# A two-layer conditioned kernel on Trainium2: another order of blocks in head and tail, a sixth buffer, and three moved steps in the loop

## What is computed

```python
# layer L0: styles scale the input channels, demod the outputs
styles = w @ (affine_w * gain).T + affine_b
dcoefs = rsqrt(sum((weight * styles)**2, axis=2) + 1e-08)
y = einsum('blc,oc->blo', x * styles, weight) * dcoefs
x = x + clip(y + bias, -256, 256)
# attention over the heads of one token: q = k = v = kx
kx = modulated_linear(x, s, k_aff_w, k_aff_b, k_w, k_b).reshape(B, N, 16, 32)
scores = einsum('bnhd,bnjd->bnhj', kx, kx) / sqrt(32)
out = einsum('bnhj,bnjd->bnhd', softmax(scores), kx).reshape(B, N, 512)
x = x + modulated_linear(out, s, o_aff_w, o_aff_b, o_w, o_b)
```

## Time and profile before

| what | value |
|---|---|
| median of the runs | 777.33 us |
| profiled execution, its own time | 782.16 us |
| its span (first to last instruction) | 780.4 us |
| granted TensorE clock, mean | 0.967 |
| busy: PE, VectorE, ScalarE | 93%, 71%, 65% |
| DMA queue of SP, share of 16 engines | 78.4% |

### The profile page before, as it was taken

One profiled execution on the slowest core, in us unless ns is written; L12 is line 12 of the kernel. 1 busy time (PEld: TensorE's weight loads), 2 busy tenths in 40 slices (PEclk: granted clock), 3 DMA queues, 4 the chain that ended last, 5 costly groups with the idle time before them and its releaser, 6 DMA issues.

```text
span 780.4 us, 21455 instructions
## 1 busy us (share of the span) xinstructions
PE 723.8 (93%) x8848; PEld 702.9 (90%) x8848; DVE 553.3 (71%) x1040; ACT 510.1 (65%) x1036; POOL 11.7 (1%) x8
## 2 busy tenths in 40 slices
PE   5999788999999999999999999999999999998676
PEld 4999678989999999999999999999999999997566
DVE  4555765778877777787787777778788777776562
ACT  4265547767776766777676677777677776675353
POOL 2300000000000000000000000000000000000000
PEclk9799898999999999999999999999999999998888
DMA  8028686898889988888878988888888889876763
GB/s 297 28 63 198 160 194 185 225 220 218 202 211 227 230 219 230 227 218 209 214 199 216 220 239 223 228 220 223 221 198 210 220 228 232 213 185 151 167 180 108
DMA packets 235778, 157.15 MB, mean 201 GB/s; under 512 B 143265, under 2 KB 225185, under 8 KB 235681
## 3 DMA queue, kind: packets, MB, share of 16 engines
q1 hardware_dynamic: 235680, 155.78, 78.4%
HBM read 71.85 MB, written 67.11 MB: 178 GB/s over the span
## 4 chain that ended last, share of the span: by engine, by line
DMA 37%; PE 28%; SPq 13%; DVE 9%; ACT 9%; issue 4%; DVEq 0%; ACTq 0%
PE lin_ps L388 21%; DMA yr<-y_turned 14%; DMA k_st<-k_turned 12%; DMA k_turned<-kx 8%; SPq L235 7%; SPq L225 4%; DVE k_rhs L676 4%; ACT y_hi L477 3%; ACT kx L468 3%; PE s_ps L426 3%; PE y_ps L444 2%; PE y_ps L411 2%; DVE p_bd L738 1%; DMA v_turned<-k_rhs 1%; SPq L249 1%
## 5 line engine op out<-in xcount | busy, mean ns | idle before, releaser
L388 PE MATMUL lin_ps<-x_hi,w_hi 128*128 128x256 f32 x1024 | 300.6, 294 | 21.5 <-ACT x_hi L477 14.5
L388 PE MATMUL lin_ps<-x_hi,w_lo 128*128 128x256 f32 x1024 | 292.8, 286 | 0.0
L388 PE MATMUL lin_ps<-x_lo,w_hi 128*128 128x256 f32 x1024 | 292.6, 286 | 0.0
L388 PEld LDWEIGHTS lin_ps<-x_hi,w_hi 128*128 128x128 f32 x1024 | 196.9, 192 | 35.1 <-issue 29.3
L388 PEld LDWEIGHTS lin_ps<-x_lo,w_hi 128*128 128x128 f32 x1024 | 197.8, 193 | 0.0
L388 PEld LDWEIGHTS lin_ps<-x_hi,w_lo 128*128 128x128 f32 x1024 | 197.2, 193 | 0.0
L388 PE MATMUL lin_ps<-y_hi,w_hi 128*128 128x256 f32 x512 | 147.6, 288 | 12.0 <-DVE y_lo L626 7.9
L388 PE MATMUL lin_ps<-y_lo,w_hi 128*128 128x256 f32 x512 | 146.7, 287 | 0.0
L388 PE MATMUL lin_ps<-y_hi,w_lo 128*128 128x256 f32 x512 | 146.5, 286 | 0.0
L477 ACT ACTIVATE x_hi<-x,style 128x256 fp32r<-128x256 f32 x256 | 115.1, 499 | 36.9 <-DVE x L697 27.1
L626 DVE SCALAR_TENSOR_TENSOR x_lo<-x,style,x_hi 128x256 fp32r<-128x256 f32 x256 | 109.5, 480 | 10.7 <-ACT x_hi L477 10.6
(11 more groups left out here) (48 smaller groups left out, 667.8 us busy)
## 6 DMA issues: line engine op xcount, KB each, us to landing
x<-xT SPq DMA_DIRECT2D x32, 512.0 KB, 6.0
k_turned<-kx SPq DMA_DIRECT2D x32, 512.0 KB, 3.6
k_st<-k_turned SPq DMA_DIRECT2D x128, 128.0 KB, 4.0
k_bd<-k_rhs SPq DMA_DIRECT2D x128, 128.0 KB, 2.4
v_turned<-k_rhs SPq DMA_DIRECT2D x32, 512.0 KB, 6.6
k_v<-v_turned SPq DMA_DIRECT2D x128, 128.0 KB, 3.7
y_turned<-y SPq DMA_DIRECT2D x128, 128.0 KB, 3.2
yr<-y_turned SPq DMA_DIRECT2D x32, 512.0 KB, 5.0
```

The lines of the kernel that those rows point to most:

```text
L388: mm = pe.matmul(lin_ps[:, n % NLB, 0:T], w[:, k, m * P:(m + 1) * P], r[:, k, :], start=(q == 0), stop=(q == len(passes) - 1))
```

## The change

Head: L0(4) and L0(5) come earlier on PE (L0(4) ahead of scores(1), L0(5) ahead of pv(1)), and O(1), K(5), scores(4) and pv(3) are written out; the loop begins at i = 6 instead of 5. Since L0(5) now comes before `finish(0)`, there are six buffers of x1, and `l0_out(c)` waits for `finish(c-6)` instead of `finish(c-5)`. SP's, ScalarE's and VectorE's heads are reordered with it. Tail: the loop ends one iteration earlier (i = 29); K(30) comes right after two blocks of O(26), L0(31) right after K(30), ahead of scores(29) and pv(28), and K(31) before the other two blocks of O(26). Loop: VectorE makes the first half of x1 ahead of `normalise`, the first low half right after, `turn_k` after both halves of x1, `spread_probabilities` after both low halves; ScalarE runs `spread_some` after both high halves of x1 instead of before `l0_out(i, 3)`. No instruction's work changes, and there are as many of each kind.

```diff
-    NX1 = DEPTH + 1
+    NX1 = DEPTH + 2
+    FIRST_LOOP = DEPTH + 2
...
-            + blocks(K, 2) + one("scores", 1) + blocks(K, 3) + one("pv", 0) + blocks(L0, 4) + one("scores", 2)
-            + blocks(K, 4) + one("pv", 1) + blocks(O, 0) + one("scores", 3) + one("pv", 2))
-        pe_program += [step for i in range(DEPTH + 1, last) for step in pe_steps(i)]
+            + blocks(K, 2) + blocks(L0, 4) + one("scores", 1) + one("pv", 0) + blocks(K, 3) + one("scores", 2)
+            + blocks(L0, 5) + one("pv", 1) + blocks(K, 4) + blocks(O, 0) + one("scores", 3) + one("pv", 2)
+            + blocks(O, 1) + blocks(K, 5) + one("scores", 4) + one("pv", 3))
+        pe_program += [step for i in range(FIRST_LOOP, last - 1) for step in pe_steps(i)]
         pe_program += (
-            blocks(L0, last) + blocks(O, last - 4, [0, 1]) + blocks(K, last) + one("scores", last - 1)
-            + one("pv", last - 2) + blocks(O, last - 4, [2, 3]) + blocks(O, last - 3) + one("scores", last)
-            + one("pv", last - 1) + blocks(O, last - 2) + one("pv", last) + blocks(O, last - 1) + blocks(O, last))
+            blocks(L0, last - 1) + blocks(O, last - 5, [0, 1]) + blocks(K, last - 1) + blocks(L0, last)
+            + one("scores", last - 2) + one("pv", last - 3) + blocks(K, last) + blocks(O, last - 5, [2, 3])
+            + one("scores", last - 1) + one("pv", last - 2) + blocks(O, last - 4) + one("scores", last)
+            + one("pv", last - 1) + blocks(O, last - 3) + blocks(O, last - 2, [0, 1]) + one("pv", last)
+            + blocks(O, last - 2, [2, 3]) + blocks(O, last - 1) + blocks(O, last))
...
                 if m == 0 and c >= NX1:
-                    act.wait_ge(v_out, 2 * (c - DEPTH))
+                    act.wait_ge(v_out, 2 * (c - NX1 + 1))
...
                     (c3, evacuate_y, 0), (c3, evacuate_y, 1), (c0, l0_out, 0), (c2, exponentials), (c0, l0_out, 1),
-                    (c0, l0_out, 2), (c2, spread_some), (c0, l0_out, 3), (c0, x1_hi_of, 0),
-                    (c4, o_out, 0), (c0, x1_hi_of, 1), (c4, o_out, 1), (i + 1, x_hi_of, 0),
+                    (c0, l0_out, 2), (c0, x1_hi_of, 0), (c0, l0_out, 3), (c4, o_out, 0), (c0, x1_hi_of, 1),
+                    (c2, spread_some), (c4, o_out, 1), (i + 1, x_hi_of, 0),
...
-                    (c2, normalise), (c0, make_x1, 0), (c2, spread_probabilities), (c1, turn_k), (c0, make_x1, 1),
-                    (c0, x1_lo_of, 0), (c0, x1_lo_of, 1), (c4, finish, 0), (c2, turn_v),
+                    (c0, make_x1, 0), (c2, normalise), (c0, x1_lo_of, 0), (c0, make_x1, 1), (c1, turn_k),
+                    (c0, x1_lo_of, 1), (c2, spread_probabilities), (c4, finish, 0), (c2, turn_v),
```

More of the change, by code:

```diff
@@ L307, in _ @@
             k_from_dram(2)
+            load_x(6)
             spread_k(2)
             v_to_dram(2)
+            y_to_dram(0)
             k_to_dram(3)
+            y_from_dram(0)
             v_from_dram(2)
             k_from_dram(3)
-            y_to_dram(0)
             spread_k(3)
-            y_from_dram(0)
-            load_x(6)
+            load_x(7)
             v_to_dram(3)
             y_to_dram(1)
+            k_to_dram(4)
             y_from_dram(1)
-            for i in range(DEPTH + 1, N):
+            v_from_dram(3)
+            k_from_dram(4)
+            spread_k(4)
+            v_to_dram(4)
+            store(0, 0, 1)
+            y_to_dram(2)
+            y_from_dram(2)
+            store(1, 0, 1)
+            for i in range(FIRST_LOOP, last - 1):
                 k_to_dram(i - 1)
@@ L326, in _ @@
                 y_from_dram(i - 3)
-                if i < N - 2:
-                    load_x(i + 2)
+                load_x(i + 2)
                 v_to_dram(i - 1)
[L330 to L333, removed]
+                store(i - 4, 0, 1)
+            k_to_dram(last - 2)
+            v_from_dram(last - 3)
+            k_from_dram(last - 2)
+            y_to_dram(last - 4)
+            spread_k(last - 2)
+            y_from_dram(last - 4)
+            v_to_dram(last - 2)
+            k_to_dram(last - 1)
+            v_from_dram(last - 2)
+            k_from_dram(last - 1)
+            y_to_dram(last - 3)
+            spread_k(last - 1)
+            y_from_dram(last - 3)
+            v_to_dram(last - 1)
             k_to_dram(last)
@@ L336, in _ @@
             k_from_dram(last)
+            store(last - 5, 0, 1)
             y_to_dram(last - 2)
@@ L593, in _ @@
[L593 to L597, removed]
@@ new lines, in _ @@
+                (3, k_out, 0), (1, exponentials), (0, evacuate_y, 0), (0, evacuate_y, 1), (3, k_out, 1),
+                (3, k_out, 2), (3, k_out, 3), (4, x1_hi_of, 0), (4, x1_hi_of, 1), (2, even_scores), (5, l0_out, 0),
+                (1, spread_some), (5, l0_out, 1), (2, exponentials), (5, l0_out, 2), (5, l0_out, 3),
+                (0, y_hi_of, 0), (4, k_out, 0), (0, y_hi_of, 1), (1, evacuate_y, 0), (1, evacuate_y, 1),
+                (4, k_out, 1), (2, spread_some), (4, k_out, 2), (4, k_out, 3), (5, x1_hi_of, 0), (0, o_out, 0),
@@ L614, in _ @@
                 (last, o_out, 0), (last, o_out, 1), (last, o_out, 2), (last, o_out, 3)]
[L615 removed]
+            for c, step, *args in act_head + [s for i in range(FIRST_LOOP, last - 1) for s in act_steps(i)] + act_tail:
                 step(c, *args)
@@ new lines, in _ @@
+                (2, merge_scores), (2, subtract_maxima), (5, make_x1, 0), (1, spread_probabilities), (3, turn_k),
+                (5, make_x1, 1), (2, normalise), (0, y_lo_of, 0), (0, y_lo_of, 1), (2, spread_probabilities),
+                (2, turn_v), (5, x1_lo_of, 0), (5, x1_lo_of, 1), (0, finish, 0), (4, turn_k), (6, x_lo_of, 0),
+                (6, x_lo_of, 1), (0, finish, 1), (3, merge_scores), (3, subtract_maxima), (1, y_lo_of, 0),
+                (1, y_lo_of, 1), (3, normalise), (1, finish, 0), (3, spread_probabilities), (3, turn_v),
```

89 lines of the change are left out of this document (49 added, 40 removed).

## The result

Over 20 runs of each kernel the change takes 784.58 us against 779.79: ratio 1.0059 [1.0031, 1.0086], about 5 us slower. The profiled execution has 790.96 us of its own time and a span of 789.2, 6.4 above its median. It is compared with before from key turn 0 on, because 5.6 us of its length arose ahead of any moved block.

| stretch | before | after | difference | forecast |
|---|---|---|---|---|
| start to key turn 0 | 62.85 | 68.48 | +5.63 | 0 |
| key turns 0 to 2 | 31.16 | 33.73 | +2.57 | 0 |
| 2 to 3 | 16.56 | 20.06 | +3.50 | +4.2 |
| 3 to 5 | 52.98 | 56.51 | +3.53 | about 0 |
| 5 to 29 (24 turns) | 521.20 | 524.69 | +3.49 | +0.5 |

The account below looks back on a forecast made before the run. A ring of transfers through SP, ScalarE and VectorE, not PE, sets the loop's 21.72 us turns. Head +4.4, loop +0.5, tail -11.5 take 780.4 to 773.8; the -6.6 put on the median 777.33 gives 770.7 us, range 760 to 784.

Parts of the forecast that it names:

- The loop, +0.5: Whole loop: ring of transfers unchanged, VectorE's order shifts a little; +0.5 us, bounds -8 and +7.
- That is under 21.72, so it acts only in the turns that were faster than 21.2: Loop: a new ring over VectorE alone sums to 21.2 us, so it rarely acts against turns of 21.72.
- +9.34: Loop: earliest start of the key turn on VectorE, 9.34 us after L0's first matmul, where it came at +8.17 before.
- the upper bound I had named: Loop: if the rings mix badly and add 0.3 us a turn, +7 us.
- My fourth rival: Loop: the new ring over VectorE sets the pace at 22.3 us a turn, +14, giving 784.2 us; chance 0.16.
- the ring of transfers: Loop: key turn, `spread_k`'s issues, yr, y's high parts, kx, next key turn; sums to 21.94 us, left unchanged.
- the wait of K for `o_out`: Loop: K's second block waits for `o_out(i-4, 1)` behind `spread_some`, ready at +13.3 where PE wants +13.1.
- The head, +4.4: Head: later key turns and PE standing 11 us before O(1) cost +4.4 us, bounds -6 and +9.
- Key turn 2 keeps its place in time: Head: key turn 2 does not move, its chain being the same and VectorE free just before; 0 us.
- with y(1)'s read between, I take 11.3: Head: the keys' trip to key turn 4 takes 11.3 us, against 10.93 in the old head, so 134.5.
- The tail, -11.5: Tail: kx(31) leaves 6.9 us after key turn 30, its trip takes 9.9; -11.5 us, bounds -16 and -5.
- The sixth buffer: Six buffers of x1: no cost, as the wait for `finish(c-6)` is met an iteration earlier than the old one.

Follow-up runs that it names:

- e1: Kernel before with six buffers and only the loop's new VectorE and ScalarE order: 782.08 us against 775.10, ratio 1.0090.
- e4: Kernel before with six buffers and `y_from_dram(i-3)` issued ahead of `spread_k(i-1)` in SP's loop: 763.48 us against 775.10, ratio 0.9850.
- e8: Kernel before with six buffers, the new tail, and `y_from_dram(i-3)` ahead of `spread_k(i-1)` in SP's loop: 756.58 us against 775.78, ratio 0.9752.
- e10: Changed kernel with `y_from_dram(i-3)` ahead of `spread_k(i-1)` in SP's loop: 772.09 us against 778.54 for the kernel before, ratio 0.9920.
- e9: Changed kernel with `o_out`'s second part ahead of `spread_some` in ScalarE's loop: 781.94 us against 778.54 for the kernel before, ratio 1.0056.
- e11: Kernel before with six buffers and new head, y issues behind `k_from_dram`, `load_x(6)` behind those: 782.39 us against 778.54, ratio 1.0046.
- e2: Kernel before with six buffers and only the new tail: 766.75 us against 775.10, ratio 0.9895.
- e16: Kernel before with six buffers, old order, key turn moved behind `make_x1`'s second half: 786.04 us against 777.18, ratio 1.0116.
- e15: Changed kernel, key turn ahead of `make_x1`'s second half, `o_out`'s second part ahead of `spread_some`: 792.11 us against 777.18 for the kernel before, ratio 1.0178.

## Why the prediction was wrong

Forecast 770.7 (range 760 to 784); it is 784.58, and +4.8 where I had -6.6.

- **The loop, +0.5.** The failed step is "That is under 21.72, so it acts only in the turns that were faster than 21.2". A turn takes the longest of chains that vary from turn to turn, so a chain whose mean is under the period still costs in the turns where it is the last to end. I had worked out the key turn's earliest start, +9.34 (measured 9.23) against +8.17, and used it only for how far PE may run ahead. With it later and the softmax chain as long as the trip of the keys, the key turns that didn't wait for keys went from 7 to 13 of 21, and the last link of the ring from 9.7 to 10.1 us. Alone that is +7.0 (e1), the upper bound I had named, 0.27 a turn in eight traces. Which of the two chains has how much of it stays open. My fourth rival (a ring over VectorE) named one of the two, though its ring is not VectorE's alone but passes through the wait for yr. That its 784.2 us is nearly the measured 784.58 is luck, since it had +14 for the loop and left head and tail as forecast.
- **That the ring of transfers bounds the loop** was right: e4, e8 and e10 take 21.1 to 21.4 once yr leaves ahead of `spread_k`. So was the wait of K for `o_out`: +13.3 against +13.1 forecast, about 0.3 a turn measured in e10. It cost nothing beside the ring (e9).
- **The head, +4.4.** "Key turn 2 keeps its place in time" failed: 2.57 later, with `load_x(6)` beside k_st(2)'s landing. e11 moved that load and the y issues together and got 1.2 of it back, so how much the load has is not settled. The stretch to key turn 3 was sized well (+4.2 forecast, 3.50 measured). The second step that failed is "with y(1)'s read between, I take 11.3": kx(4) was issued 9.15 after key turn 3 (8.4 forecast), and its trip to key turn 4 took 13.94. Together that is 3.4 us more, and it makes O(1)'s wait 14.11 for 11. From key turn 4 to 5 it is 33.4, as forecast. From key turn 0 to 5 the trace has +9.6, the runs with the head alone +7.0 by their ratio.
- **The tail, -11.5.** The mechanism held: key turn 31 is 18.38 after key turn 30 (about 17 forecast, 25.76 before). Too large were kx(31)'s 6.9 after the key turn (8.03 measured) and the trip's 9.9 (10.35); the trace has -9.9, e2 alone -8.1.
- **The sixth buffer** at nothing: never run alone, but e2, e4 and e8 have it and are faster.

The sum was thus wrong through three mis-sized terms that all fell on the same side: the head (5.2 more than forecast in the trace), the loop (3.0 more in the trace, 6.5 by e1), and the tail, which gave 1.6 to 3.4 less.

## What to carry to other kernels

A step that waits for a transfer has two times: when the transfer lands, and the earliest at which its own queue lets it start. If both are within a microsecond, price the later start by how many turns reach it, not by whether the mean is under the period. Then follow back what sets that earliest start: here part of it came out of the same ring, through the softmax. And when a variant hits its forecast number, look in its trace for the forecast's mechanism too; in e16 it was another. Look for the ring first and ask which link is an order and not work: here one line in the transfer queue was worth more than the whole rewritten order. And orders of two engines that hand halves to each other are one table; half of it alone cost up to 13%.

## What was unexpected of the hardware

The granted clock in the first 60 us varies from run to run although PE is busy nearly throughout, 0.87 and 0.66 in the windows above, and key turn 0 varies with it from 60.4 us (e10, 0.91) to 68.5 (after, 0.66), as much as the effects studied here.

One execution of e15 took 3854.8 us, the other four 789 to 796. Its largest group of instructions (busy us, mean ns of one, idle time before):

```profile
L413 PE MATMUL lin_ps<-x_hi,w_hi 128*128 128x256 f32 x1024 | 1063.7, 1039 | 5.0 <-DVE w_lo L686 5.0
```

A matmul took 1039 ns there and 294 in the kernel after, while VectorE was busy for about as long as ever (555.5 us for 551.8). The profile page has no row for the granted clock in this execution, nothing else in the trace says why, and it did not come again.
